# State-space layer: input products of seven of sixteen states by ScalarE on turned tiles, sums accumulated by transposes

## What is computed

```python
dt = softplus(dt @ W_dt.T + b_dt)         # (tokens, 384)
A  = -exp(A_log)                          # (384, 16)
def step(h, inp):
    dA = exp(dt_t[..., None] * A)                             # decay
    h = dA * h + (dt_t * x_t)[..., None] * B_t[:, None, :]    # input product, scan
    y = einsum('bdn,bn->bd', h, C_t)                          # readout, sum over the states n
y = (ys + xc * D_param) * silu(z)
out = y @ W_out.T
```

## Time and profile before

| | |
|---|---|
| median of 3 runs | 4595.27 us (4592.28 to 4600.84) |
| the profiled execution's own time | 4601.28 us |
| its span, first to last instruction | 4599.5 us |
| mean granted clock of TensorE | 0.949 |
| busy share of the span: PE, DVE, ACT, POOL | 90%, 71%, 52%, 70% |
| state-space phase | from about 1100 to about 3765 us of the span |

### The profile page before, as it was taken

One profiled execution on the slowest core, in us unless ns is written; L12 is line 12 of the kernel. 1 busy time (PEld: TensorE's weight loads), 2 busy tenths in 40 slices (PEclk: granted clock), 3 DMA queues, 4 the chain that ended last, 5 costly groups with the idle time before them and its releaser, 6 DMA issues. The chain is left out here.

```text
span 4599.5 us, 63372 instructions
## 1 busy us (share of the span) xinstructions
PE 4145.6 (90%) x17184; PEld 2234.8 (49%) x17184; DVE 3250.3 (71%) x5016; ACT 2413.6 (52%) x4880; POOL 3215.3 (70%) x1671
## 2 busy tenths in 40 slices
PE   7988958996999999999999999999999974999994
PEld 5666646672344344344334434433433434666773
DVE  5777762121899999999899999999989986112124
ACT  3566632223766766666676666667667544222221
POOL 3233213441999999999999999999999971444441
PEclk7999987997999999999999999999999987999997
DMA  1000023451343333433333333333333321344466
GB/s 34 25 21 23 15 64 87 122 151 52 108 119 116 120 112 112 124 112 120 120 115 112 112 115 121 113 115 116 122 112 115 111 85 49 109 117 118 134 185 227
DMA packets 264754, 478.66 MB, mean 104 GB/s; under 512 B 37044, under 2 KB 174084, under 8 KB 264548
## 3 DMA queue, kind: packets, MB, share of 16 engines
q1 hardware_dynamic: 235776, 403.02, 27.8%
q0 software_dynamic: 28032, 73.17, 6.4%
q10 hardware_dynamic: 740, 0.49, 0.0%
HBM read 409.60 MB, written 41.81 MB: 98 GB/s over the span
## 5 line engine op out<-in xcount | busy, mean ns | idle before, releaser
L1818 POOL TENSOR_TENSOR m_xh<-m_u,m_Bb 128x1536 f32<-128x1536 f32 x512 | 1776.9, 3539 | 58.1 <-DVE m_u L1689 44.9
L1745 PE MATMUL bank<-m_xh,ident 128*128 128x512 f32 x3072 | 1459.7, 611 | 36.3 <-POOL m_xh L1807 36.3
L1787 DVE TENSOR_TENSOR_SCAN bank<-bank,m_xh 128x512 f32<-128x512 f32 x864 | 1039.0, 1216 | 45.1 <-ACT bank L1774 41.9
L1774 ACT ACTIVATE bank<-m_dt,m_Ac 128x508 f32<-128x508 f32 x1536 | 1024.7, 683 | 38.4 <-DVE m_xh L1787 38.4
L1745 PEld LDWEIGHTS bank<-m_xh,ident 128*128 128x128 f32 x3072 | 577.2, 194 | 828.6 <-issue 737.1
L1787 DVE TENSOR_TENSOR_SCAN m_xh<-bank,m_xh 128x512 f32<-128x512 f32 x672 | 787.7, 1207 | 71.5 <-ACT bank L1774 66.0
L1807 POOL TENSOR_TENSOR m_xh<-m_xh,m_Cb 128x1536 f32<-128x1536 f32 x224 | 791.2, 3532 | 4.8 <-DVE m_xh L1787 4.5
L1798 DVE TENSOR_TENSOR m_xh<-bank,m_Cb 128x512 f32<-128x512 f32 x864 | 580.8, 672 | 9.8 <-DMA m_Cb<-BC_rows 9.8
L1204 ACT ACTIVATE f1t_h<-bank,f1t_b 128x512 f32<-128x512 f32 (+1 forms) x276 | 142.8, 589 | 471.3 <-PE bank L1239 471.3
L1593 PE MATMUL bank<-m_xp,m_dg 128*128 128x512 f32 x768 | 352.4, 601 | 3.7 <-DVE m_u L1689 1.4
L1134 POOL DMA_INDIRECT rows_y<-f1t_y,f1t_home x142 | 140.3, 988 | 272.7 <-DVE f1t_y L1175 243.4
(11 more groups left out here) (367 smaller groups left out, 6002.0 us busy)
## 6 DMA issues: line engine op xcount, KB each, us to landing
m_Bb<-BC_rows SPq DMA_DIRECT2D x256, 512.0 KB, 4.9
m_Cb<-BC_rows SPq DMA_DIRECT2D x256, 512.0 KB, 4.1
f1t_w<-f_w SPq DMA_DIRECT2D x46, 576.0 KB
m_r<-m_dt POOLq DMA_DIRECT2D x32, 768.0 KB, 7.4
f1t_w1a<-f_w SPq DMA_DIRECT2D x46, 384.0 KB
f0t_w<-f_w SPq DMA_DIRECT2D x22, 576.0 KB
f1c_yg<-rows_y SPq DMA_DIRECT2D x16, 768.0 KB, 8.3
f1t_w1b<-f_w SPq DMA_DIRECT2D x92, 96.0 KB
```

Of the source, the lines that this page charges most:

```text
L1745: mm = pe.matmul(bank[:, c, :], K.ident[:, :], xh[n % NX][:, c, :], start=False, stop=(d == 1 and n == NS - 1))
L1774: act.activation(o[:, :, lo:hi], seqs(dt[d][:, c, :])[:, :, lo:hi], ACT.Exp, scale=Ac[:, c, n:n + 1]).then_inc(s_dA, 1)
L1787: dve.tensor_tensor_scan(o, bank[:, RING[d][p], way], xh[n % NX][:, c, way], 0.0, ALU.mult, ALU.add).then_inc(s_h, 1)
L1818: pool.tensor_tensor(xh[n % NX][:, :, :], u[d][:, :, :], Bb[q % RB][:, n % QN, :].unsqueeze(1).to_broadcast([P, DC, TOK]), ALU.mult).then_ ...
```

## The change

1. **Turned products.** For the states in `TURNED` = 2, 4, ..., 14 the product u x B no longer comes from POOL. Once a half, PE transposes u (`pe_uT`, 24 transposes of 128x128 a group) and ACT copies the result to `uT` (`act_uT`), so that tokens lie on the partitions. There B is one number for each partition, and ACT multiplies a piece of 128x384 by it (`act_part`, 4 pieces a state). PE transposes the pieces back (`pe_back`, 4 transposes a unit), into the unit's ring bank, LEAD = 2 units ahead of the unit. The decay of such a unit goes to `xh` in SBUF instead, and the scan takes its two inputs the other way round. `pe_BT`, `act_BT` turn B.
2. **Readouts.** `BY_POOL` has 9 states of d = 0 and 8 of d = 1, all seven turned ones among them, where it had 8 and 6. So POOL reads 17 states a group where it read 14, and DVE 15 where it read 18. (The words of the change, four readouts moved from GpSimd to VectorE, do not describe the step from this kernel.)
3. **Sums.** `pe_sum` accumulates by four transposes of 128x128 instead of one float32 matmul of 512 columns. The sums therefore stand turned in banks 0 to 2; `pe_D` is four matmuls of 128 columns, and at the end of a group ACT copies the sums out (`act_yt`) and PE turns them back (`pe_yT`), ahead of `dve_y`.
4. **Edges.** The zeros ahead of the decays go: `act_sp` writes 1e30 into dt at the edges (6 small copies a group), so that the exponential gives zero there, and a decay is 512 columns wide.
5. **Places.** `POS` is rewritten: PE steps and the ACT steps that wait for them now stand two units apart in most places; `pe_sp0` moves from 26, 36, 40 to 31, 33, 35.
6. **SP.** B comes one state at a time, 9 rows a half, in 3 buffers.

```diff
-        BY_POOL = (0, 3, 4, 5, 10, 12, 13, 14), (0, 6, 9, 10, 11, 14)
+        BY_POOL = (2, 3, 4, 6, 8, 10, 11, 12, 14), (2, 4, 6, 7, 8, 10, 12, 14)
+        TURNED = (2, 4, 6, 8, 10, 12, 14)
...
+        NX, AHEAD, LAG, LEAD = 8, 2, 3, 2
+        PART = (-4, -3, -3, -2)
...
+            def pe_uT(pe, b):
...
+                for k in range(G):
+                    j, c = divmod(b * G + k, DC)
+                    mm = pe.transpose(bank[:, NB, k * P:(k + 1) * P], u[d][:, c, j * P:(j + 1) * P], K.ident[:, :])
...
-            mm = pe.matmul(bank[:, c, :], K.ident[:, :], xh[n % NX][:, c, :], start=False, stop=(d == 1 and n == NS - 1))
+            for j in range(G):
...
+                mm = pe.matmul(sums(j, c), xh[n % NX][:, c, j * P:(j + 1) * P], K.ident[:, :], start=False, stop=closes,
+                               is_transpose=True, skip_group_check=True)
...
+        def act_yt(act, g, b):
+            act.wait_ge(s_red, (g + 1) * 2 * UNITS)
+            act.copy(yt[:, b, :], bank[:, b, :]).then_inc(s_yt, 1)
+
+        def pe_yT(pe, g, c):
+            pe.wait_ge(s_yt, (g + 1) * DC)
+            for j in range(G):
+                b, k = place(j, c)
+                mm = pe.transpose(bank[:, c, j * P:(j + 1) * P], yt[:, b, k * P:(k + 1) * P], K.ident[:, :])
...
-            if back or pb // DC not in BY_POOL[d] or d == 0 and p == ROWS_TO:
-                act.copy(o[:, :, edge:edge + 1], none[:, :].unsqueeze(2))
-            act.activation(o[:, :, lo:hi], seqs(dt[d][:, c, :])[:, :, lo:hi], ACT.Exp, scale=Ac[:, c, n:n + 1]).then_inc(s_dA, 1)
+            if n in TURNED:
+                if c == 0 and (later(g, d) or n >= NX):
+                    act.wait_ge(s_red, ((g * 2 + d) * NS + n - NX + 1) * DC)
+                o = xh[n % NX][:, c, :]
+            else:
+                bank_free(act, g, d, p)
+                o = bank[:, RING[d][p], :]
+            act.activation(o, dt[d][:, c, :], ACT.Exp, scale=Ac[:, c, n:n + 1]).then_inc(s_dA, 1)
...
+        def act_part(act, g, d, n, j):
+            if j == 0:
+                if later(g, d) or n > TURNED[0]:
+                    act.wait_ge(s_turned, turned(g, d, n) * DC)
...
+            flat = uT[:, :, :].rearrange("p b x -> p (b x)")
+            act.activation(turn[:, j, :], flat[:, j * DC * P:(j + 1) * DC * P], ACT.Copy,
+                           scale=BT[d][:, j, TURNED.index(n):TURNED.index(n) + 1]).then_inc(s_part, 1)
+
+        def pe_back(pe, g, d, p):
+            n, c = divmod(p, DC)
+            if c == 0:
+                pe.wait_ge(s_part, turned(g, d, n) * G + G)
+            bank_free(pe, g, d, p)
+            for j in range(G):
+                mm = pe.transpose(bank[:, RING[d][p], j * P:(j + 1) * P], turn[:, j, c * P:(c + 1) * P], K.ident[:, :])
+            mm.then_inc(s_turned, 1)
...
-                    if c == 0 and not (end and n >= NS - AHEAD):
+                    if c == 0 and at_step(g, d, n + AHEAD)[2] in OWN and not (end and n >= NS - AHEAD):
                         pool_dBx(pool, *at_step(g, d, n + AHEAD))
```

More of the change, by code:

```diff
@@ L1409, in mamba_phase @@
         dve_reads = lambda g, d, n: g * (of_dve(0, NS) + of_dve(1, NS)) + d * of_dve(0, NS) + of_dve(d, n)
+        made = lambda g, d, n: (g * 2 + d) * NO + sum(k < n for k in OWN)
+        turned = lambda g, d, n: (g * 2 + d) * NT + TURNED.index(n)
         of_q = lambda q: range(q * QN, (q + 1) * QN)
@@ L1768, in act_decay, with bank_free @@
+            act.activation(o, dt[d][:, c, :], ACT.Exp, scale=Ac[:, c, n:n + 1]).then_inc(s_dA, 1)
+        def bank_free(eng, g, d, p):
+            back, db, pb = before_in_bank(d, p)
             if d == 0 and p == ROWS_TO and not (isinstance(g, int) and g == NG - 1):
[L1769 removed]
+                eng.wait_ge(s_added, g * 2 + 4)
             elif back == 0 or later(g, d):
[L1771 to L1773 removed]
@@ L1789, in dve_read @@
+            if n in TURNED:
+                dve.wait_ge(s_turned, turned(g, d, n) * DC + c + 1)
+                fade, add = add, fade
+            elif c == 0:
+                dve.wait_ge(s_dBx, made(g, d, n) + 1)
+            o = xh[n % NX][:, c, way] if n in BY_POOL[d] else bank[:, RING[d][p], way]
+            dve.tensor_tensor_scan(o, fade, add, 0.0, ALU.mult, ALU.add).then_inc(s_h, 1)
         def dve_read(dve, g, d, p):
@@ L1869, in sums_at @@
                 upto = p + 1 - LAG * DC
-                begun = sum(p >= at for at in POS["pe_D0"])
-                if carry and begun < DC:
-                    upto = min(upto, begun)
-                now = list(range(done, min(upto, done + 2)))
+                if carry:
+                    begun = sum(p >= at for at in POS["pe_D0"])
+                    upto = min(3 * (p + 1) - LAG * DC, 0) if begun < DC else upto
+                now = list(range(done, min(upto, done + 3)))
                 plan.append(now)
@@ L1915, in main @@
                     carry = d == 0 and later(g)
+                    if p + LEAD < UNITS and (p + LEAD) // DC in TURNED:
+                        pe_back(pe, g, d, p + LEAD)
+                    if carry:
+                        for c, at in enumerate(POS["pe_yT"]):
+                            if at == p:
+                                pe_yT(pe, g - 1, c)
                     if carry and p in POS["pe_D0"]:
@@ L1930, in after @@
                             pe_sum(pe, NG - 1, 1, n, c)
+                    for c in range(DC):
+                        pe_yT(pe, NG - 1, c)
                     for i in two:
@@ L1938, in main, with after @@
                     act_decay(act, g, d, p)
-                program(act, "act", main, lambda act: None, lambda act: None)
+                    for n in TURNED:
+                        for j, at in enumerate(PART):
+                            if n * DC + at == p:
+                                act_part(act, g, d, n, j)
+                    if d == 0 and later(g):
+                        for b, at in enumerate(POS["act_yt"]):
+                            if at == p:
+                                act_yt(act, g - 1, b)
+                def after(act):
+                    for b in range(DC):
+                        act_yt(act, NG - 1, b)
+                program(act, "act", main, lambda act: None, after)
             @block.gpsimd
```

162 lines of the change are left out of this document (102 added, 60 removed), and 6 rows, old and new, of the table POS.

## The result

The changed kernel takes 5014.8 us (median of 4 runs, 5010.9 to 5019.7), the kernel before beside it 4595.0 us. The ratio is 1.091 (95% interval 1.089 to 1.093), +420 us. The forecast was 4423 us with a range up to 4545 us, so its sign was wrong.

The account below looks back on a forecast made before the run. POOL was taken as the bound at 163.5 us a group; DVE's 143.7 plus 8.5 of waits gave 152.2. Over 16 groups 181 us, less about 9 at start and end, net -172: 4423 us, range 4325 to 4545.

Parts of the forecast that it names:

- The works: Forecast work per engine after the change, a group: POOL 121.7 us, DVE 143.7, ACT 140.1; a piece 587 ns.
- PE's forecast load by spacing: PE's work a group, counted by the spacing of its records: from about 148 to about 132 us (130 to 141).
- POOL sets the period: In the state-space phase before, POOL was the bound: 97.9% busy, at 163.5 us a group.
- The 8.5 us of waits: Waits charged to DVE a group after the change, a choice with bounds 3 and 15 us; the step trusted least.
- The forecast of 152.2: Period a group after the change: DVE's work of 143.7 us plus 8.5 us of waits, 11.3 less than 163.5.
- The places were counted as a gain: Longer distances between chain steps should shrink PE's 4.0 us wait for the accumulating DMA and ACT's 17.7 us behind it.
- as much as PE's burst once a half: Upper bound for DVE's waits, 15 us a group: those of before plus a PE burst each half.
- ACT's idle time was taken for slack: ACT, idle a third of the time, would take added work up to 140.1 us a group, 4 us behind DVE.
- A: Rival: ACT becomes the bound, 140 us plus 18 of waits, period 158, 4516 us; chance 0.20.
- B: Rival: the waits go, DVE runs at 143.7 + 3 = 146.7 us a group, 4335 us; chance 0.14.
- C: Rival: PE becomes the bound at half clock in sparse stretches, period 167, about 4660 us, slower; chance 0.12.
- The rule on the clock: Skill's rule that transposes don't engage PE's full clock; the prediction held that the trace disagrees, costing little where PE has slack.

Follow-up runs that it names:

- (6): The kernel before with POOL's products of states 2, 4, ..., 14 made for one channel slice of three: 4509.8 us, ratio 0.981.
- (10): The changed kernel without ACT's pieces, without pe_back and without DVE's wait for it: 4686.3 us.
- (9): The changed kernel without ACT's 56 pieces; PE turns back a buffer of zeros: 4723.7 us.
- (4): The changed kernel with each of ACT's pieces 64 instead of 384 columns wide: 4864.7 us.
- (11): The kernel before with the changed edges, and the readout of state 4 of d = 0 moved from POOL to DVE: 4602.3 us, ratio 1.0014.
- (1): The changed kernel with pe_back ahead of the chain steps of its place in PE's queue: 4993.0 us.
- (5): The changed kernel with two turn buffers for ACT's pieces, and slice 0's weights used for slices 1 and 2 to make room: 4925.8 us.
- (12): The changed kernel with one tap of the convolution instead of four: 4906.6 us.
- run 7: The kernel before with only the changed kernel's list of places: 4778.0 us, ratio 1.038.
- 8: The kernel before with both the turned sums and the changed kernel's places, no turned products: 4768.2 us.
- run 2: The changed kernel with the sums again done by one matmul of 512 columns a unit, without act_yt and pe_yT: 5119.7 us.
- run 3: The kernel before with only the sums turned, by accumulating transposes: 4661.6 us, ratio 1.015.

## Why the prediction was wrong, point by point

**Where the 191.0 us come from.** The runs line up (us a group; in another order the steps could come out otherwise):

| kernel | period | step |
|---|---|---|
| before | 163.5 | |
| POOL relieved alone (6) | 157.1 | -6.4 |
| the change without its products (10) | 169.3 | +12.2 |
| with backs, no pieces (9) | 172.0 | +2.7 |
| with short pieces (4) | 181.7 | +9.7 |
| the kernel after | 191.0 | +9.3 |

The step of 12.2 holds all else that the change does; the run with the places alone gives 11.9 and the one with places and turned sums 11.1, so most of it is put down to the places. That these numbers are one thing is argued, not isolated. The last two steps are ACT's 56 pieces: 0.17 us of period for each piece that has only a sixth of its width, and as much again for the rest of the width. By ACT's busy time, which is 28.3 us with all pieces and 13.7 with the short ones, that is 0.71 us of period for each us at first and 0.64 after.

**The works: right.** POOL 121.7 forecast, 123.6 measured; DVE 143.7 and 146.6; ACT 140.1 and 138.2; a piece 587 and 604 ns; exchanged scan inputs free. In ACT's sum two misses cancel, which is luck: its 56 pieces add 28.3 us of busy time and not 32.9 (9), since they overlap their neighbours, and taking the edge copies away gave 4.1 us and not 7.7 (11). The transposes of the sums follow each other at (1.09 - 0.29) / 7 = 0.114 us (eight at 2317.38 in the timeline of the kernel after), between the two values taken. PE's forecast load by spacing, 132 us, can't be compared with its recorded 156.8, in which modelled ends overlap.

**POOL sets the period: right, and worth less than it looked.** The run with POOL alone relieved gives 157.1, with 8 us of idle on DVE. The forecast of 152.2 is that less about DVE's 6.1 us of readouts. The 8.5 us of waits fit the kernel before with less POOL, and not the changed one.

**The 8.5 us of waits: the step that failed.** It was named as the one trusted least, with 3 and 15 as bounds; the trace shows 44.4, of which 16.1 are for `pe_back` and 24.9 for ACT. Three things were wrong in it.

- *The places were counted as a gain* ("there are now 6 and 8 units in place of 3 and 9"). I looked at the wait for the accumulating DMA only. That wait did go, from 57.5 us in 14 groups to none, and ACT's behind it fell from 240.6 to 172.0. But the run with the places alone costs 11.9 us a group. In the kernel before, `pe_conv0` stands 3 to 7 units ahead of `act_conv0` and the ends of the chain are spread. My reading, which no run isolates pair by pair, is that two units are less than PE's lateness at the long steps, and that ACT, a strict queue, holds the decays behind each such wait.
- *The new loop was priced as if PE were rarely late.* In the timeline above `pe_back` starts 5.2 us after its data. The bound "as much as PE's burst once a half" allowed it twice a group; DVE's scans waited for `pe_back` 159 times in 14 groups, 225.0 us. And when that wait was taken away (1), or that for the buffer (5), 1.3 and 5.9 us of 16 came back and the rest moved on.
- *ACT's idle time was taken for slack.* ACT had 54.3 us idle in a group of 163.5, so 29 us more looked as if they fit. But of the idle before, 240.6 + 115.2 + 52.3 + 48.2 = 456 us in 14 groups, 33 a group, are ACT's waits for PE's chain steps: links of a dependent sequence that passes between PE and ACT, not room for work. ACT's idle kept its sum and changed its make-up. All its waits for DVE, mostly for a free bank, fell from 19.5 to 6.1 us a group, so that part was room; those for PE rose from 34.3 to 43.4, of which 16.5 are the new one for `pe_back`. What is laid on ACT beyond that lengthens the period; hence 0.64 us of period for each us of ACT's width (4), and 0.41 for each of PE's chain (12), while 30 us less on POOL gave 6.4, or 0.21.

**The rivals.** A (ACT becomes the bound) named the mechanism nearest to what the runs show, the strict queue in which "one wait there delays decays", but left 18 us of ACT's waits where 52.8 stay, and so ended on the faster side. That 138.2 + 52.8 is the period proves nothing for it, as any engine's busy and idle time add up to the period; runs 4 and 9 are what speaks for it, and by run 4 ACT's load is not the whole bound. B needed waits of 3 us; the opposite came. C (PE at half clock) had the sign, and one of the two things it said the profile would show: DVE's scans do wait for PE's transposes, 225.0 us in 14 groups. The other, a clock below 0.8, did not come; it is 0.91. Nor do period and clock go together: from run 7 to 8 the clock falls from 0.96 to 0.87 and from run 9 to 10 from 0.97 to 0.90, and neither is slower for it, while PE has less work in both. Single long steps do run at half clock (the gate matmuls above), which is part of how late `pe_back` gets; how much of the 27.5 us that is was not measured apart.

**The rule on the clock.** The prediction said that the trace of before shows the clock rising on transposes alone. At that place real matmuls had run until 36.67 us, just ahead of the 12 transposes, so it shows less than that. The kernel after shows more: there are stretches in which PE does nothing but transposes for over 14 us, and the granted clock stays at the higher of its levels throughout:

```profile
1589.70:1604.38 14.68, 10.69 (x92) 9.72 (x91) 13.36 (x14) 13.47 (x26) 13.15 (x5) 1.00 0.35 114
```

The Trainium skill, page "TensorE: Matmul & The Clock Gate", Part 4, says that full clock does not engage for them. By this stretch that does not hold as stated. Over the phase three quarters of PE's records are transposes and the clock is 0.91. Still, replacing dense matmuls by transposes went with a lower clock: 0.97 in run 2 and 0.91 in the kernel after, 0.98 in the kernel before and 0.88 in run 3.

**What stays open.** How the pieces' first 9.7 us divide between ACT's time and new waits; what the lower clock costs by itself; and whether other places would suit the changed kernel, which is the obvious next trial, as the places cost most of the step of 12.2. By my reading of the code the places of the kernel before can't be used as they are, since PE's steps stand there up to several units ahead of the ACT steps that they wait for (`pe_dt0` at 12, `act_pj` at 15), and a `pe_back` behind such a step is needed by the scans that free the banks for ACT's decays ahead of 15. Neither this nor other places were tried. No run that computes the whole layer beat the kernel before; the only faster one (6) leaves work out.

## What to carry to other kernels

An engine's idle time is room for more work only as far as it isn't a wait in a sequence that goes back and forth with another engine. Before loading it, sort its waits: here those that ended with a bank's release were room, and those for the next step of a chain mostly were not. Then, before building the whole change, run two cheap kernels: one that only relieves the bound (it gives what that relief can win while the rest stays; here 6.4 us of 163.5), and one that only moves the steps to their new places (here it cost 11.9, nearly twice that).

## What the runs showed of the hardware

- Less work for PE can go with a slower PE: the granted clock of the phase went from 0.98 to 0.88 with the sums turned (3), while PE was recorded busy 82% of it after 97%, and to 1.00 with POOL relieved (6), PE busy 99%.
- A decay of 512 columns takes 716 ns into SBUF and 682 ns into PSUM. A scan with its output in SBUF takes 1207 ns with the decay in PSUM (before) and 1211 ns with the product there (after).
- Taking one wait away left the sum of idle time almost as it was: DVE's idle is 44.4 us a group in the kernel after and (2655.81 - 2055.99) / 14 = 42.8 with the backs first (1).
